# Four graph layers in one kernel: layer 2's one-hot, transposes and aggregation in bf16, with the message as three bf16 pieces

## What is computed

```python
msg_in = jnp.concatenate([h[src], h[dst], e], axis=-1)      # 128 + 128 + 64 features of an edge
messages = jax.nn.silu(msg_in @ w1 + b1) @ w2 + b2
gates = jax.nn.sigmoid(msg_in @ wg + bg)
messages = messages * gates
agg = jax.ops.segment_sum(messages, dst, num_segments=n)
deg = jax.ops.segment_sum(jnp.ones((dst.shape[0],), h.dtype), dst, num_segments=n)
agg = agg / jnp.maximum(deg, 1.0)[:, None]
h_new = jax.nn.silu(jnp.concatenate([h, agg], axis=-1) @ wu + bu)
```

## Time and profile before

| | |
|---|---|
| median of 3 runs | 5813.93 us (5810.95 to 5816.22) |
| profiled execution, device time | 5813.95 us |
| its span, first to last instruction | 5812.3 us |
| lies around the span | 1.65 us |
| mean granted TensorE clock | 0.759 |
| PE busy / PEld busy | 4224.1 us (73%) / 3052.0 us (53%) |
| DVE / ACT / POOL busy | 3311.8 (57%) / 1685.6 (29%) / 3782.6 us (65%) |
| edge stage of layer 2 | from 3202 to 4600 us of the span |

### The profile page before, as it was taken

One profiled execution on the slowest core, in us unless ns is written; L12 is line 12 of the kernel. 1 busy time (PEld: TensorE's weight loads), 2 busy tenths in 40 slices (PEclk: granted clock), 3 DMA queues, 4 the chain that ended last, 5 costly groups with the idle time before them and its releaser, 6 DMA issues. The chain is left out here.

```text
span 5812.3 us, 106638 instructions
## 1 busy us (share of the span) xinstructions
PE 4224.1 (73%) x20886; PEld 3052.0 (53%) x20887; DVE 3311.8 (57%) x10595; ACT 1685.6 (29%) x5074; POOL 3782.6 (65%) x3395
## 2 busy tenths in 40 slices
PE   0178878788874334444447999999999868888888
PEld 0156666666663333333335677777777645555555
DVE  4265655555553633333336555555555568888886
ACT  0132222222221000000002333333333445555554
POOL 2178888888886077777771665555655257777774
PEclk9865555555555655555557999999999989999999
DMA  5755555555555211111111333333333123333332
GB/s 140 217 77 70 70 71 70 70 70 70 71 70 97 58 51 52 52 52 52 52 52 57 108 98 98 98 99 98 99 97 99 46 60 58 58 57 57 57 57 54
DMA packets 741221, 442.03 MB, mean 76 GB/s; under 512 B 434953, under 2 KB 675443, under 8 KB 740602
## 3 DMA queue, kind: packets, MB, share of 16 engines
q0 software_dynamic: 217824, 319.22, 26.8%
q1 hardware_dynamic: 523322, 121.99, 10.6%
HBM read 355.73 MB, written 116.63 MB: 81 GB/s over the span
## 5 line engine op out<-in xcount | busy, mean ns | idle before, releaser
L632 POOL DMA_INDIRECT G<-table,src_it x2496 | 2415.7, 968 | 1196.1 <-issue 694.0
L608 POOL DMA_INDIRECT sums<-work,idx x832 | 1295.8, 1557 | 282.8 <-issue 186.3
L1295 DVE TENSOR_TENSOR big<-bank,big 128x129 f32 (+2 forms) x2496 | 886.3, 355 | 930.8 <-PE bank L710 512.1
L710 PE MATMUL bank<-G,oh 128*128 128x129 f32 x1664 | 428.6, 439 | 628.9 <-DMA G<-table,src_it 628.9
L744 PE MATMUL bank<-work 128*128 128x128 f32 x1664 | 621.5, 475 | 212.6 <-DVE work L1342 185.9
L710 PEld LDWEIGHTS bank<-G,oh 128*128 128x128 f32 x1664 | 372.7, 329 | 684.7 <-issue 479.8
L849 PE MATMUL bank<-big,oh 128*128 128x320 f32 x1664 | 592.8, 461 | 110.9 <-DVE big L1295 110.7
L955 ACT ACTIVATE work<-bank,work 128x128 f32<-128x128 f32 x832 | 306.2, 368 | 1082.0 <-PE bank L736 1082.0
L744 PEld LDWEIGHTS bank<-work 128*128 128x128 f32 x1664 | 406.5, 303 | 402.6 <-DVE work L1342 399.7
L736 PE MATMUL bank<-big,work 128*128 x1664 | 577.0, 449 | 0.1
L1282 DVE TENSOR_TENSOR oh<-iota,rel_it 128x512 f32<-128x512 f32 x625 | 428.6, 686 | 157.2 <-issue 88.2
(11 more groups left out here) (226 smaller groups left out, 6382.8 us busy)
## 6 DMA issues: line engine op xcount, KB each, us to landing
G<-e_src SPq DMA_DIRECT2D x832, 64.0 KB, 3.1
G<-table,src_it POOLq DMA_INDIRECT x2496, 2.5
work<-e_a SPq DMA_DIRECT2D x832, 32.0 KB
e_a<-in_edge_attr_dram POOLq DMA_DIRECT2D x1, 25000.0 KB, 102.0
sums<-work,idx POOLq DMA_INDIRECT x832
work<-e_a SPq DMA_DIRECT2D x832, 4.0 KB
work<-e_a SPq DMA_DIRECT2D x832, 2.0 KB
sums<-big POOLq DMA_DIRECT2D x4, 3264.0 KB
```

What stands on the lines that cost most here:

```text
L608: pool.indirect_dma_start(sums[k % COPIES], bass.IndirectOffsetOnAxis(ap=idx[:, k:k + 1], axis=0), z_out[:, k, :], None, compute_op=ALU.ad ...
L632: pool.indirect_dma_start(G[:, k, 0:wid], None, tab, bass.IndirectOffsetOnAxis(ap=src_it[:, n:n + 1], axis=0)).then_inc(quad_in[layer - 1] ...
L710: mm = t.matmul(bank[4 * o + j][:, 0:wid], oh[:, n, :], G[:, n, 0:wid], start=True, stop=True)
L1295: v.tensor_tensor(to, ps, to, ALU.add).then_inc(EDGE[layer]["acc_done"], 1)
```

## The change

Layer 2's one-hot is written in bf16 into the memory of `oh`, which then holds eight quads (`oh2`). The one-hot's transposes take bf16 with a bf16 identity, into half of bank 0. The message, 128 x 512 float32 per quad, is split: ACT copies it to bf16 (high), DVE subtracts that in place (rest), ACT copies the rest to bf16 (middle), DVE subtracts again and writes bf16 (low). The aggregation multiplies the bf16 one-hot with the three pieces, twelve matmuls of 128 columns a quad in place of four float32 ones. DVE's order within a body is new: L1393, rest, two additions, one-hot, low, two additions, message. PE and DVE have eight bodies in a loop turn in place of four. The semaphores of `attr3` become ones that layer 0 has used already, and PE's loop starts after `ident_b` is written.

```diff
-        attr3 = [sem(f"attr3_{k}") for k in range(8)]
+        attr3, ATTR3_BEFORE = attr_in[0:8], 16 * (ITEMS // RING)
 (PE, edges2)
-                            t.transpose(bank[0][:, j * P:(j + 1) * P], oh[:, k % 4 * 4 + j, :], ident[:])
+                            t.transpose(bank[0][:, 0:256].bitcast(BF16)[:, j * P:(j + 1) * P], oh2[:, k % 8 * 4 + j, :], ident_b[:])
...
-                        pe.wait_ge(ph["msg_done"], q - 2)
+                        pe.wait_ge(ph["low_done"], q - 2)
                         for j in range(4):
-                            mm = t.matmul(bank[6 + (k - 3) % 2][:, j * P:(j + 1) * P], oh[:, (k - 3) % 4 * 4 + j, :],
-                                          msg2[:, (k - 3) % 2, j, :], start=True, stop=True)
+                            for piece in range(3):
+                                mm = t.matmul(bank[6 + (k - 3) % 2][:, j * P:(j + 1) * P], oh2[:, (k - 3) % 8 * 4 + j, :],
+                                              pieces2[(k - 3) % 2][:, piece, j * P:(j + 1) * P], start=(piece == 0), stop=(piece == 2))
                         mm.then_inc(ph["agg_done"], 1)
-                quad_steps(pe, 3, top, body, 4)
+                quad_steps(pe, 3, top, body, 8)
 (ACT, edges2, between L968 and the SiLU)
+                    if live(3):
+                        act.wait_ge(ph["rest_done"], q - 2)
+                        a.activation(pieces2[(k - 3) % 2][:, 1, :], flat3(msg2[:, (k - 3) % 2, :, :]), ACT.Copy).then_inc(ph["mid_done"], 1)
 (ACT, edges2, at the end of the body)
+                    if live(2):
+                        act.wait_ge(ph["msg_done"], q - 1)
+                        if live(4):
+                            act.wait_ge(ph["agg_done"], q - 3)
+                        a.activation(pieces2[k % 2][:, 0, :], flat3(msg2[:, k % 2, :, :]), ACT.Copy).then_inc(ph["hi_done"], 1)
-                quad_steps(act, 2, lambda item: None, body, 4)
+                quad_steps(act, 3, lambda item: None, body, 4)
 (DVE, edges2: the additions and the one-hot leave their old places; after L1393 come)
+                    if live(3):
+                        o = (k - 3) % 2
+                        dve.wait_ge(ph["hi_done"], q - 2)
+                        m = flat3(msg2[:, o, :, :])
+                        v.tensor_tensor(m, m, pieces2[o][:, 0, :], ALU.subtract).then_inc(ph["rest_done"], 1)
+                    if live(4):
+                        dve.wait_ge(ph["agg_done"], q - 3)
+                        add(0)
+                        add(1)
+                    if live(0) and not (isinstance(q, int) and q == QUADS - 1):
+                        onehot4(ph, q + 1, k + 1, oh2, 8)
+                    if live(3):
+                        dve.wait_ge(ph["mid_done"], q - 2)
+                        v.tensor_tensor(pieces2[o][:, 2, :], m, pieces2[o][:, 1, :], ALU.subtract).then_inc(ph["low_done"], 1)
+                    if live(4):
+                        add(2)
+                        add(3)
                     if live(2):
                         dve.wait_ge(ph["m_done"], q - 1)
+                        dve.wait_ge(ph["gate_done"], q - 1)
                         if live(4):
-                            dve.wait_ge(ph["agg_done"], q - 3)
-                        dve.wait_ge(ph["gate_done"], q - 1)
+                            dve.wait_ge(ph["low_done"], q - 3)
...
+                v.tensor_copy(ident_b[:], ident[:]).then_inc(ident_ready, 1)
+                quad_steps(dve, 4, top, body, 8)
```

More of the change, by code:

```diff
@@ L92, in gnn_layers @@
         ident, ones, iota = sb("ident", [P, P]), sb("ones", [P, P]), sb("iota", [P, P])
-        ones_b = sb("ones_b", [P, P], BF16)
+        ones_b, ident_b = sb("ones_b", [P, P], BF16), sb("ident_b", [P, P], BF16)
         tri, iota_p, icol = sb("tri", [P, P]), sb("iota_p", [P, 1]), sb("icol", [P, CHUNKS])
@@ L132, in gnn_layers @@
         a64 = view(5632, [8, 64])
+        pieces2 = [view(c, [768]).bitcast(BF16).rearrange("p (c f) -> p c f", f=512) for c in (2048, 6144)]
+        oh2 = oh[:, :, :].rearrange("p a b -> p (a b)").bitcast(BF16).rearrange("p (a b) -> p a b", b=P)
         spare3 = big[:, NBT * L3W:BIGW]
@@ L193, in gnn_layers @@
         quad_in = [[sem(f"quad_in{layer}_{k}") for k in range(4)] for layer in (1, 2, 3)]
-        attr3 = [sem(f"attr3_{k}") for k in range(8)]
+        attr3, ATTR3_BEFORE = attr_in[0:8], 16 * (ITEMS // RING)
+        ident_ready = sem("ident_ready")
         fc_zero, fc_in, fc_ready = sem("fc_zero"), sem("fc_in"), sem("fc_ready")
@@ L209, in gnn_layers @@
                 Phase("l2", "oh_ready t_done ev_done pre_done add_done sil_done gate_done "
-                            "t2_done ev2_done m_done msg_done agg_done acc_done"),
+                            "t2_done ev2_done m_done msg_done hi_done rest_done mid_done low_done agg_done acc_done"),
                 Phase("l3", "oh_ready t_done ev_done h_done hid_done w_done "
@@ L750, in edges2 @@
                 regs = [pe.alloc_register(f"qblk{k}") for k in range(RING)]
+                pe.wait_ge(ident_ready, 1)
                 def top(item):
@@ L838, in body @@
                             pe.wait_ge(ph["ev_done"], q)
-                        pe.wait_ge(attr3[k % 8], landed(128, 8, q, k, 0))
+                        pe.wait_ge(attr3[k % 8], landed(128, 8, q, k, 0) + ATTR3_BEFORE)
                         t.transpose(bank[0][0:32, 0:P], a8q[:, k % 8, :, :].rearrange("p a f -> p (a f)"), ident[:]).then_inc(ph["t_done"], 1)
@@ L980, in body @@
                             act.wait_ge(ph["pre_done"], q)
-                        a.activation(ohT2.rearrange("p a b -> p (a b)"), bank[0][:, :], ACT.Copy)
+                        a.activation(ohT2.rearrange("p a b -> p (a b)"), bank[0][:, 0:256].bitcast(BF16), ACT.Copy)
                         a.activation(eT2.rearrange("p a b -> p (a b)"), bank[4][:, 0:256], ACT.Copy).then_inc(ph["ev_done"], 1)
-                quad_steps(act, 2, lambda item: None, body, 4)
+                    if live(2):
[4 more added lines that the diff above has]
+                quad_steps(act, 3, lambda item: None, body, 4)
                 barrier(act)
@@ L1278, in node_tables, with onehot4 @@
                 barrier(dve)
-            def onehot4(ph, q, k):
-                v.tensor_tensor(oh[:, k % 4 * 4:k % 4 * 4 + 4, :], iota[:].unsqueeze(1).broadcast_to([P, 4, P]),
+            def onehot4(ph, q, k, oh=oh, slots=4):
+                v.tensor_tensor(oh[:, k % slots * 4:k % slots * 4 + 4, :], iota[:].unsqueeze(1).broadcast_to([P, 4, P]),
                                 rel_it[:, bass.ds(q * 4, 4)].unsqueeze(2).broadcast_to([P, 4, P]),
@@ L1378, in body, with add @@
                 def body(q, k, live):
-                    if live(4):
-                        dve.wait_ge(ph["agg_done"], q - 3)
-                        for j in range(4):
-                            add_item(2, regs[k % 4 * 4 + j], bank[6 + k % 2][:, j * P:(j + 1) * P],
-                                     4 * q - 16 + j if live(5) or j else None)
+                    def add(j):
+                        add_item(2, regs[k % 4 * 4 + j], bank[6 + k % 2][:, j * P:(j + 1) * P],
+                                 4 * q - 16 + j if live(5) or j else None)
                     if isinstance(q, int) and q == 0:
-                        onehot4(ph, 0, 0)
+                        onehot4(ph, 0, 0, oh2, 8)
                     if live(1):
```

## The result

The kernel after takes 6115.57 us (median of 4 runs, 6111.91 to 6115.94) where the kernel before, on the same chip, takes 5815.07: 1.0517 times as long, 95% interval 1.0498 to 1.0535. The change costs 300 us. The prediction was 6103 us, with a range of 6000 to 6250.

A forecast was written before the change was run, and what follows sets the result against it. PE bounds layer 2's edge stage now; the ring through DVE would replace it: 7.80 + 0.25 for boundaries = 8.05 us a quad against 6.66, 1.39 x 208 = 289 us on 5814, so 6103 us, range 6000 to 6250.

The forecast's parts named there:

- the SiLU's start: On ACT: SiLU, held up by rest and middle, was to start 1.3 us after L1393's end.
- The ring through DVE: From one L765 start to the next through PE's first part, DVE's steps to low and the aggregation: 7.80 us, binding.
- PE's first part: On PE, from the start of L765 until DVE's L1393 starts: 2.90 us.
- The twelve passes: PE's aggregation in bf16: passes 0.06 us apart, 0.72 us in all, 0.18 less than the float32 passes.
- The rival with 0.112 each: The aggregation's twelve passes cost 0.112 us each: 8.67 us a quad, 6232 us; 15 in 100.
- The boundaries: PE's block-number read and the loop's branches: 0.25 us a quad, with 0.1 and 0.35 as bounds.
- the aggregation's 0.72 covers part: PE's 1.109 us register read each fourth quad is partly hidden by the aggregation; at least 0.4 us shows.
- The clock: PE's clock in layer 2's edge stage stays 1.00; a rival had it fall to 0.50, 6830 us, 5 in 100.
- The ring through ACT: From L765 through rest, middle, SiLU, tanh and ACT's copies back to PE: 7.40 us, shorter than DVE's by 0.4.
- the ACT ring binds: Rival: DVE's steps shorter or additions later than put, so ACT's ring sets 7.65 us a quad, 6020 us; 15 in 100.
- The transposes: PE's L788 in bf16 saves 0 to 0.22 us, worth nothing because L798 waits for ACT's L968 anyway.
- PE stays the limit: Rival: low is done in time and the aggregation's 0.18 us a quad is gained, 5777 us; 4 in 100.

The follow-up runs named there:

- late_agg: The changed kernel with PE's aggregation, and DVE's additions with it, one body later; 6651.52 us, 1.0072 of the kernel before on that chip.
- late_mid: late_agg with ACT's middle copy also behind its copies for PE and DVE's low behind the message; 6619.04 us, 1.0018 of the kernel before.
- late_all_2: The kernel of late_all again, on a chip where the kernel before takes 5810.93 us; 5647.23 us, 0.9719.
- fill_after: The changed kernel with eight extra bf16 matmuls a quad on PE ahead of its wait for low; 6756.52 us, 1.0138 of the kernel before.
- fill_after_2: The kernel of fill_after once more, on another chip; 6690.24 us against 6597.9 for the kernel before, 1.0137.
- oh_behind_low: The changed kernel with DVE's one-hot moved behind low; 6734.61 us against 6668.8 for the kernel before, 1.0104.
- half_tr_before: The kernel before with two of the four one-hot transposes left out; 6663.04 us against 6668.8, 0.9989.
- late_all: late_mid with PE's aggregation also ahead of the second product and ACT's copies for PE ahead of SiLU and tanh; 6589.54 us, 0.9984.

## Why the prediction was right, point by point

- **The time and the cause held.** Two rings through DVE and ACT take the place of PE's own work, DVE's the longer. PE's wait for low (1.14 us in the quad shown) and the SiLU's start (1.17 us after L1404's end; 1.3 was predicted, though the prediction's own sum gives 5.36 - 4.19 = 1.17) are in the trace, and *late_agg*, *late_mid* and *late_all_2* take the loss away as the rings go.
- **The ring through DVE was put 0.30 too long**: 7.80, measured 7.50. PE's first part took the 2.90. From L1404 to L812 it was 3.92 us, not 4.18: two additions took 0.63 to the start of the one-hot, where I had 0.86. I had charged both with a wait for one another (0.43 each); the second doesn't pay one to the next, unrelated instruction. The one-hot took 0.60 to low's start, where I had taken its recorded 0.69. From low's start to L812 it was 0.88, 0.05 more than I had. The twelve passes took 0.66, not 0.72.
- **The twelve passes**: (0.83 - 0.22) / 11 = 0.055 us apart, the lower of my bounds and the half of L765's spacing. Each has its own weight load, recorded at 98 ns in the median, and they are hidden. The rule of the Trainium skill ("TensorE: Matmul & The Clock Gate", "Back-to-back issue gap": about 81 ns for a pair at 128 columns) does not hold for this stream; by it the twelve would have taken 0.97 us. The row of the nearest kind was the better guide. The rival with 0.112 each fell with it.
- **The boundaries were put too low**: 0.25 a quad, measured 0.36. The step that failed is "the aggregation's 0.72 covers part" of PE's register read, with "at least 0.4 us" left to show. 0.97 of its 1.11 us show, so that hardly 0.15 are covered. Branches do halve, but the one that is left costs 0.57 us each eighth quad, a term that I had not sized. My upper bound, 0.35, was just below the sum.
- **The clock was sized as all or nothing.** I gave a loss of it 5 in 100, at 6830 us, and the forecast none. It came in some 40 of 207 quads, some 50 us. The forecast's "the stage's clock is 1.00" was wrong (0.95). *fill_after* and *fill_after_2*, with no such quad, bear the size out. Why these quads and not others, and why *late_agg*, whose PE is busy for 81% between 3500 and 4500 us, kept 1.00 there, is open; *oh_behind_low*, busy for the same 81%, had eight such quads.
- **The errors cancel**: -0.30 + 0.11 + 0.25 = 0.06 us a quad, 12 us, which is what lies between 6103 and 6115.57. The closeness of the total is luck in part; a range of 250 us was not too wide.
- **The ring through ACT** was put at 7.40. *late_agg* showed 7.5, on a chip of the second kind: there L769 starts 0.26 us after L990's end, where I had 0.14. So the rival "the ACT ring binds" (6020 us) would have been nearly the same ring; its time was low by the boundaries and the clock.
- **The transposes are worth nothing**, as predicted. L802 waited 73 us for L973 in after, L798 31 us in before; *half_tr_before* shows the mechanism alone. In *late_all_2* other work stands in that wait, so that the saving can count.
- **PE stays the limit** (5777 us, 4 in 100) fell: 0.88 us more on PE cost 0.12 us or less. Its figure was small for what the pieces can give, because it kept the old order: with the steps moved, 5647 us was there.

## What to carry to other kernels

When a step between two engines gets longer by others on a third, don't ask whether those engines have busy time to spare, but how many bodies lie between who makes the value and who takes it. DVE with 4.7 us of work in an 8 us quad was in the ring that set the pace here because PE took the value of the same body. With one body more between them PE no longer waited for it at all, and with ACT's steps and PE's moved as well the added work cost nothing. Write down each ring (from a start to the same start of the next body), put the sum beside the engine's own work, and count a register read (0.97 of 1.11 us here) or a branch nearly in full when it stands behind the ring's wait. And a saving in front of a wait is nothing until something else is moved into the wait.

## What the runs showed of the hardware that I had not expected

- bf16 passes of 128 columns with a weight load each start 0.055 us apart (L812, L792 and L803), as near as their columns let one expect from L765; the loads, 98 ns each as recorded, don't show.
- TensorE's clock can be at 1.2 GHz in single quads of a stage and at 2.4 in the others: some 40 of 207 here, from 3577 us on the same three of every 16, with 1.1 us and 0.33 us of waiting in every quad of both kinds. Eight more matmuls in the longer wait brought 1.00 in the whole stretch.
- The same kernel takes 5811 us on one chip and 6598 to 6669 on another, with the first DVE step of a quad 1.06 instead of 0.05 us after the PE step that it waits for, and ACT's L968 0.53 instead of 0.04. A small edit that is timed only on the second kind can look worthless though it is not: *late_all* was 0.9984 there and 0.9719 here.
- Additions of 128 x 128 start 0.43 us apart when each waits for the one before; when nothing depends on it, the next instruction starts sooner, two additions and all in 0.63.
